# Angle attention on one core: weights as nodes by edges on ScalarE, turned back on TensorE, lags up to six

## What is computed

```python
def _agnn_layer(h, src, dst, beta, num_nodes):
    h_norm = h * jax.lax.rsqrt(jnp.sum(h * h, axis=-1, keepdims=True) + EPS)
    cos = jnp.sum(h_norm[src] * h_norm[dst], axis=-1)
    logits = beta * cos
    m = jax.ops.segment_max(logits, dst, num_segments=num_nodes)
    ex = jnp.exp(logits - m[dst])
    denom = jax.ops.segment_sum(ex, dst, num_segments=num_nodes)
    alpha = ex / (denom[dst] + EPS)
    msg = alpha[:, None] * h[src]
    return jax.ops.segment_sum(msg, dst, num_segments=num_nodes)
h = feats
for i in range(N_LAYERS):      # 4
    h = _agnn_layer(h, src, dst, betas[i], num_nodes)
    h = jax.nn.relu(h)
```

## Time and profile before

| | us |
|---|---|
| timed runs, median of 3 | 11036.81 (11017.5 to 11073.92) |
| profiled execution | 11119.13 |
| its span, first to last instruction | 11117.1 |

### The profile page before, as it was taken

The page is one execution under the profiler, slowest core; times in us unless marked ns, Lnnn a source line. Parts: engine busy times, 40 slices in busy tenths (PEclk is TensorE's granted clock), DMA queues, the critical chain, the costliest instruction groups (busy, mean ns, idle before and its releaser), DMA issues. The chain is left out here.

```text
span 11117.1 us, 155608 instructions
## 1 busy us (share of the span) xinstructions
PE 7197.0 (65%) x34292; PEld 5512.2 (50%) x34293; DVE 5850.1 (53%) x21199; ACT 2582.1 (23%) x6846; POOL 5289.8 (48%) x5498
## 2 busy tenths in 40 slices
PE   0013334434474927886886886887598878887887
PEld 0013334423353826775775775776355545554554
DVE  6012233331113246776666666777576756675767
ACT  0000000000011211221221221221345544544544
POOL 2766666646612125554554554554344434444443
PEclk9986666666667968998998997998666666666666
DMA  3101123343425923353334334334222422232323
GB/s 145 50 14 40 40 54 83 83 68 91 89 19 176 364 89 87 81 80 72 78 79 70 79 79 70 81 80 63 62 69 66 66 62 66 68 60 71 69 68 59
DMA packets 614773, 886.43 MB, mean 80 GB/s; under 512 B 285681, under 2 KB 423153, under 8 KB 613400
## 3 DMA queue, kind: packets, MB, share of 16 engines
q0 software_dynamic: 241344, 609.84, 26.2%
q1 hardware_dynamic: 373336, 275.69, 8.2%
HBM read 757.50 MB, written 134.32 MB: 80 GB/s over the span
## 5 line engine op out<-in xcount | busy, mean ns | idle before, releaser
L1529 POOL DMA_INDIRECT hs<-tab_agnn,rec x1952 | 1899.2, 973 | 1782.6 <-PE psV L1679 655.8
L1963 POOL DMA_INDIRECT hs<-tab_gat,rec x1464 | 1388.1, 948 | 1591.3 <-DVE msg L2032 1156.7
L2139 PE MATMUL psV<-msg,ohf 128*128 128x260 f32 x2928 | 1264.9, 608 | 0.0
L2001 DVE CUSTOM_DVE_ANT_0 cand<-psL,neg 128x512 f32<-128x512 f32 x1464 | 975.6, 685 | 345.7 <-issue 230.9
L1655 PE MATMUL psG<-HN,ohT 128*128 x3904 | 1030.0, 411 | 65.9 <-issue 40.4
L1679 PE MATMUL psV<-hs,pr 128*128 128x258 f32 x3904 | 1056.5, 418 | 5.9 <-DVE pr L1589 5.9
L1550 DVE CUSTOM_DVE_ANT_0 prod<-psG,hs 128x256 f32<-128x256 f32 x1952 | 828.3, 480 | 415.6 <-issue 208.0
L2139 PEld LDWEIGHTS psV<-msg,ohf 128*128 128x128 f32 x2928 | 882.4, 315 | 199.1
L1655 PEld LDWEIGHTS psG<-HN,ohT 128*128 128x128 f32 x3904 | 778.4, 210 | 175.2 <-issue 74.2
L645 PE MATMUL psT<-ident,oh 128*128 128x128 f32 x488 | 120.4, 393 | 1129.0 <-DVE oh L611 1001.7
L1679 PEld LDWEIGHTS psV<-hs,pr 128*128 128x128 f32 x3904 | 752.6, 203 | 106.3 <-DVE pr L1589 8.2
(11 more groups left out here) (324 smaller groups left out, 13041.6 us busy)
## 6 DMA issues: line engine op xcount, KB each, us to landing
w<-in_L_gnn_w SPq DMA_DIRECT2D x224, 512.0 KB, 5.8
fwd_d<-acc SPq DMA_DIRECT2D x10, 3172.0 KB
fw<-fwd_d SPq DMA_DIRECT2D x122, 260.0 KB
hs<-tab_agnn,rec POOLq DMA_INDIRECT x1952
hs<-tab_gat,rec POOLq DMA_INDIRECT x1464
rec<-rec_d SPq DMA_DIRECT2D x1220, 8.0 KB
b<-in_L_gnn_b SPq DMA_DIRECT2D x113, 128.0 KB, 6.5
x<-xbuf SPq DMA_DIRECT2D x112, 128.0 KB, 6.1
```

Of the source, the lines that this page charges most:

```text
L1529: nc.gpsimd.indirect_dma_start(out=hs[:, j, g, :], out_offset=None, in_=k.tab_agnn, in_offset=bass.IndirectOffsetOnAxis(ap=rec[:, j, g, 0: ...
L1963: nc.gpsimd.indirect_dma_start(out=hs[:, j, g, :], out_offset=None, in_=k.tab_gat, in_offset=bass.IndirectOffsetOnAxis(ap=rec[:, j, g, 0:1 ...
L2001: V.tensor_tensor_reduce(cand[:, m, :], psL[:, m, :], neg[:, h2, :], 1.0, -BIG, ALU.add, ALU.max, mt[:, h2, m:m + 1]).then_inc(s_lt, 1)
L2139: mm = nc.tensor.matmul(psV[:, h4, 0:W_GAT], ohf[:, h4, g, :], msg[:, h4, g, :], start=(g == 0), stop=(g == G - 1))
```

## The change

The weights are no longer made edge by edge. VectorE's cand already holds, nodes by edges, the logit where edge and node belong together and a number near -1e30 elsewhere. ScalarE takes Exp of it with the bias -peak per node (prT, 512 columns); TensorE turns its four squares to edges by nodes (psP, in place of psQ), and ScalarE copies that to pr. tt, below, ex and the four pr on VectorE go. The running value is kept with its sign turned (low in place of peak), so that it serves as bias. neg is built with 2e30.

The lags become, for TensorE: psL of s-3, psG of s-1, psP of s-4, psT of s, psV of s-5. For VectorE: cand and mn of s-4, oh of s, df of s-4, acc of s-6, the store of s-4, prod of s-2. For ScalarE: ohT and neg of s-1, prT and rs of s-4, pr of s-5. oh, ohT, prT and prod have two buffers, neg three; psP has one, so its transposes wait for the copy of the tile before. In the graph attention three waits count their events from zero, since the angle attention no longer raises those semaphores.

Core of the diff (the lines taken out are those shown above; indents are cut):

```diff
...
-peak = sb("peak", [P, NB])
+low = sb("low", [P, NB])
...
+s_turn = sem("s_turn")
+s_oT = sem("s_oT")
...
-oh = sb("oh", [P, U, G, P], BF16)
-ohT = sb("ohT", [P, U, G, P])
-neg = sb("neg", [P, U, G * P])
-prod = sb("prod", [P, G, D])
+oh = sb("oh", [P, 2, G, P], BF16)
+ohT = sb("ohT", [P, 2, G, P])
+neg = sb("neg", [P, 3, G * P])
+prT = sb("prT", [P, 2, G * P])
+prod = sb("prod", [P, 2, G, D])
...
-tt = sb("tt", [P, 2, G])
-below = sb("below", [P, 2, G])
-ex = sb("ex", [P, 2, G])
...
-psQ = ps("psQ", [P, 512])
+psP = ps("psP", [P, G * P])
...
-            nc.vector.memset(peak[:, :], -BIG)
+            nc.vector.memset(low[:, :], BIG)
...
 blocks = Numbers(nc, dve, k.gb[:, 0, :], "block")
 def step(i, j):
...
+    now, mid_, old, add = (lagged(i, j, n) for n in (0, 2, 4, 6))
+    if old:
+        _, j4, t4 = old
+        h4 = j4 % 2
+        at = pick(low, blocks.at(j, 4))
+        dve.wait_ge(q.b, flow(t4) + 1)
+        if not (isinstance(t4, int) and t4 < 2):
+            dve.wait_ge(q.e, flow(t4 - 1))
+        dve.sem_inc(q.gate_dve, 1)
+        V.tensor_tensor_reduce(cand[:, h4, :], psL[:, :], neg[:, j4 % 3, :], 1.0, -BIG, ALU.add, ALU.max,
+                               mt[:, h4:h4 + 1]).then_inc(s_mx, 1)
+        dve.wait_ge(s_mx, own(t4) * 2 + 1)
+        V.scalar_tensor_tensor(out=mn[:, h4:h4 + 1], in0=mt[:, h4:h4 + 1], scalar=-1.0, in1=at,
+                               op0=ALU.mult, op1=ALU.min).then_inc(q.m, 1)
+    if now:
+        i0, _, t = now
+        dve.wait_ge(q.rec[j], use(i0, j) * 16 + 16)
+        if not (isinstance(t, int) and t < 2):
+            dve.wait_ge(q.t, flow(t - 1))
+        V.tensor_tensor(oh[:, j % 2, :, :], mid(k.iota[:, :], G), b3(recf[:, j, :, 1], P),
+                        ALU.is_equal).then_inc(q.oh, 1)
+    if old:
+        dve.wait_ge(q.m, flow(t4) + 1)
+        if not (isinstance(t4, int) and t4 < 2):
+            dve.wait_ge(q.rs, flow(t4 - 1))
+        dve.sem_inc(q.gate_dve, 1)
+        V.tensor_tensor(df[:, h4:h4 + 1], mn[:, h4:h4 + 1], at, ALU.subtract).then_inc(q.df, 1)
+    if add:
+        _, j6, t6 = add
+        acc = pick(k.acc, blocks.at(j, 6), slice(0, cols)).rearrange("p a c -> p (a c)")
+        dve.wait_ge(q.v, nth(t6) + 1)
+        dve.wait_ge(q.rs, flow(t6) + 1)
+        if not (isinstance(t6, int) and t6 < 1):
+            dve.wait_ge(q.u, nth(t6))
+        V.scalar_tensor_tensor(out=acc, in0=acc, scalar=rs[:, j6:j6 + 1], in1=psV[:, 0:cols],
+                               op0=ALU.mult, op1=ALU.add).then_inc(q.u, 1)
+    if old:
+        dve.wait_ge(q.df, flow(t4) + 1)
+        dve.sem_inc(q.gate_dve, 1)
+        V.tensor_copy(at, mn[:, h4:h4 + 1]).then_inc(s_mx, 1)
     if mid_:
         i2, j2, t2 = mid_
         h2 = j2 % 2
...
         dve.wait_ge(q.gather[j2], use(i2, j2) * (16 * G) + 16 * G)
         dve.wait_ge(s_g, own(t2) + 1)
+        if not (isinstance(t2, int) and t2 < 2):
+            dve.wait_ge(s_l, own(t2 - 1))
+            dve.wait_ge(q.b, flow(t2 - 1))
         for g in range(G):
...
+            ins = V.tensor_tensor_reduce(prod[:, h2, g, :], psG[:, h2, g, :], hs[:, j2, g, 0:D], hs[:, j2, g, D:D + 1],
                                          0.0, ALU.mult, ALU.add, lg[:, h2, g:g + 1])
         ins.then_inc(s_l, 1)
...
+pipeline(dve, step, 6, numbers=blocks)
 @block.scalar
 def _(act):
 def step(i, j):
...
+    last, old, done = (lagged(i, j, n) for n in (1, 4, 5))
+    if last:
+        _, j1, t1 = last
+        act.wait_ge(q.t, flow(t1) + 1)
+        if not (isinstance(t1, int) and t1 < 2):
+            act.wait_ge(s_g, own(t1 - 1))
+        nc.scalar.activation(ohT[:, j1 % 2, :, :].rearrange("p g e -> p (g e)"), psT[:, :], ACT.Copy).then_inc(s_oT, 1)
+        if not (isinstance(t1, int) and t1 < 3):
+            act.wait_ge(s_mx, own(t1 - 3) * 2 + 1)
+        nc.scalar.activation(neg[:, j1 % 3, :], psT[:, :], ACT.Copy, bias=-2 * BIG, scale=2 * BIG).then_inc(q.ev, 1)
     if old:
...
+        _, j4, t4 = old
+        h = j4 % 2
+        act.wait_ge(q.m, flow(t4) + 1)
+        if not (isinstance(t4, int) and t4 < 2):
+            act.wait_ge(s_turn, own(t4 - 1))
+        nc.scalar.activation(prT[:, h, :], cand[:, h, :], ACT.Exp, bias=mn[:, h:h + 1]).then_inc(q.e, 1)
+        act.wait_ge(q.df, flow(t4) + 1)
+        if not (isinstance(t4, int) and t4 < U):
+            act.wait_ge(q.u, nth(t4 - U + 1))
+        nc.scalar.activation(rs[:, j4:j4 + 1], df[:, h:h + 1], ACT.Exp).then_inc(q.rs, 1)
+    if done:
+        _, j5, t5 = done
+        act.wait_ge(s_turn, own(t5) + 1)
+        if not (isinstance(t5, int) and t5 < 2):
+            act.wait_ge(q.v, nth(t5 - 1))
+        nc.scalar.activation(pr[:, j5 % 2, :, :].rearrange("p g e -> p (g e)"), psP[:, :], ACT.Copy).then_inc(s_p, 1)
+pipeline(act, step, 5)
 @block.tensor
 def _(pe):
 blocks = Numbers(nc, pe, k.gb[:, 0, :], "block")
 def step(i, j):
...
+    now, last, cos, old, add = (lagged(i, j, n) for n in (0, 1, 3, 4, 5))
+    if cos:
+        _, j3, t3 = cos
+        pe.wait_ge(s_l, own(t3) + 1)
+        if not (isinstance(t3, int) and t3 < 1):
+            pe.wait_ge(q.m, flow(t3))
         for g in range(G):
...
+            mm = nc.tensor.transpose(psL[:, g * P:(g + 1) * P], lg[:, j3 % 2, g:g + 1].to_broadcast([P, P]), k.ident[:, :])
         mm.then_inc(q.b, 1)
     if last:
         _, j1, t1 = last
         b = blocks.at(j, 1)
...
+        pe.wait_ge(s_oT, own(t1) + 1)
         if not (isinstance(t1, int) and t1 < 2):
             pe.wait_ge(s_l, own(t1 - 1))
         for g in range(G):
...
+            mm = nc.tensor.matmul(psG[:, j1 % 2, g, :], ohT[:, j1 % 2, g, :],
                                   pick(HN, b, slice(None)).rearrange("p a c -> p (a c)"), start=True, stop=True)
         mm.then_inc(s_g, 1)
+    if old:
+        _, j4, t4 = old
+        pe.wait_ge(q.e, flow(t4) + 1)
+        if not (isinstance(t4, int) and t4 < 1):
+            pe.wait_ge(s_p, own(t4))
+        for g in range(G):
+            mm = nc.tensor.transpose(psP[:, g * P:(g + 1) * P], prT[:, j4 % 2, g * P:(g + 1) * P], k.ident[:, :])
+        mm.then_inc(s_turn, 1)
     if now:
         _, _, t = now
         pe.wait_ge(q.oh, nth(t) + 1)
         if not (isinstance(t, int) and t < 1):
             pe.wait_ge(q.ev, flow(t))
         for g in range(G):
...
+            mm = nc.tensor.transpose(psT[:, g * P:(g + 1) * P], oh[:, j % 2, g, :], k.identb[:, :])
         mm.then_inc(q.t, 1)
...
+    if add:
+        _, j5, t5 = add
+        pe.wait_ge(s_p, own(t5) + 1)
+        if not (isinstance(t5, int) and t5 < 1):
+            pe.wait_ge(q.u, nth(t5))
         for g in range(G):
...
+            mm = nc.tensor.matmul(psV[:, 0:cols], pr[:, j5 % 2, g, :], hs[:, j5, g, 0:cols],
                                   start=(g == 0), stop=(g == G - 1))
         mm.then_inc(q.v, 1)
...
+pipeline(pe, step, 5, numbers=blocks)
 with nc.Block() as block:
...
-    dve.wait_ge(q.q, flow(t) + 1)
+    dve.wait_ge(q.q, own(t) + 1)
-    dve.wait_ge(q.tt, flow(t) + 1)
+    dve.wait_ge(q.tt, own(t) + 1)
...
```

More of the change, by code:

```diff
@@ L1562, in step @@
[L1562 to L1566, removed]
-                            V.tensor_tensor(oh[:, j, :, :], mid(k.iota[:, :], G), b3(recf[:, j, :, 1], P),
-                                            ALU.is_equal).then_inc(q.oh, 1)
-                        if add:
-                            _, j4, t4 = add
-                            acc = pick(k.acc, blocks.at(j, 4), slice(0, cols)).rearrange("p a c -> p (a c)")
-                            dve.wait_ge(q.v, nth(t4) + 1)
-                            dve.wait_ge(q.rs, flow(t4) + 1)
-                            if not (isinstance(t4, int) and t4 < 1):
-                                dve.wait_ge(q.u, nth(t4))
-                            V.scalar_tensor_tensor(out=acc, in0=acc, scalar=rs[:, j4:j4 + 1], in1=psV[:, 0:cols],
-                                                   op0=ALU.mult, op1=ALU.add).then_inc(q.u, 1)
@@ L1578, in step @@
-                        if mid_:
-                            dve.wait_ge(q.b, flow(t2) + 1)
-                            dve.wait_ge(q.ev, flow(t2) + 1)
-                            dve.sem_inc(q.gate_dve, 1)
-                            V.tensor_tensor_reduce(cand[:, h2, :], psL[:, :], neg[:, j2, :], 1.0, -BIG, ALU.add, ALU.max,
-                                                   mt[:, h2:h2 + 1]).then_inc(s_mx, 1)
-                        def weighted(*tiles):
-                            if old:
-                                dve.wait_ge(q.e, flow(t3) + 1)
-                                for g in tiles:
-                                    ins = V.tensor_scalar(pr[:, h3, g, :], oh[:, j3, g, :], ex[:, h3, g:g + 1], None, ALU.mult)
-                                if g == G - 1:
-                                    ins.then_inc(s_p, 1)
@@ L1609, in step @@
                     def step(i, j):
-                        now, mid_, old = lagged(i, j, 0), lagged(i, j, 2), lagged(i, j, 3)
-                        if old:
```

(24 more changed lines are left out.)

57 lines of the change are left out of this document (4 added, 53 removed).

## The result

| | before | after | after / before |
|---|---|---|---|
| timed runs, median us | 11043.5 (11017.5 to 11073.9) | 11235.6 (11190.4 to 11241.6) | 1.0164 [1.0126, 1.0202] |
| span of the profiled execution, us | 11117.1 | 11232.9 | |

A forecast was written before the change was run, and what follows sets the result against it. The prediction took hand-overs between TensorE and VectorE to bound the angle attention at 6.85 us a tile; floors of 5.05 (TensorE) and 5.1 (GpSimd) were taken to a pace of 6.0, saving 399 us: 10641 us, range 10230 to 10880.

## What to carry to other kernels

Where a stage without an edit becomes slower, look at the instruction queue's packets in its loop, at the first instruction after the branch, and at short stops 128 instructions apart: the position of a loop of some 20 KB modulo 8 KB was worth 2%, more than the change itself, and must be made equal before two versions are compared. A lag counted in steps is not a cover: count for each hand-over the microseconds of work that stand between the producer's end and the consumer's start on the same engine. And read whether idle time ends in prompt or late signals before charging it to a wait: the same kernel took 5.35 us a tile on chips with prompt signals and 6.85 with late ones.

## What was not expected of the hardware

VectorE's branch back costs 0.25 us when its loop stays loaded and 2.86 us when it is fetched again, five packets of 8 KB an iteration, 54 times: 160 us in the first comparison, 223 to 255 us on the other chips (2962.2 - 2739.4 and 2992.3 - 2736.9). The late branches themselves make 141 to 162 us of that, and on the other chips the three stops of a third of a microsecond, where the loop crosses from one piece to the next, make 55 to 57. In the first comparison an iteration takes only 2.79 us more in all, so there the stops lie in time that VectorE waited anyway. And psT's signal was over 5.7 us late in one tile of twenty in the kernel before in the first comparison (one in eleven in the changed one), and 0.15 us at the same mark on the other chips; with them the whole of the same program takes 9.67 ms in place of 11.04. How much of that is the signals was not measured.
